# Routed experts of a small decoder: the expert's weights as the stationary operand of the gate and up products

## The chip, the cores and the metric

The kernel runs on one core of a Trainium2 chip. The metric is the device time of one execution in microseconds (us), lower is better. The engines that matter here are TensorE (PE in the profile, its weight loads PEld), VectorE (DVE), ScalarE (ACT), GpSimd (POOL) and SyncE (SP), which issues most transfers. Each engine has a sequencer of its own that takes its instructions in program order; the profile writes it with a q behind the engine's name (PEldq is TensorE's).

## The reference

Two decoder layers over x of 8 x 512 tokens with 256 channels: attention, cross attention and a feed-forward part each. The part that the change touches is the last one, a mixture of experts over all 4096 tokens:

```
logits = xt @ router_w.T + routing_bias          # 8 experts
topk_p, topk_idx = top_k(sigmoid(logits), 2)     # normalised to sum 1
g = einsum('th,eih->tei', xt, wg)                # H = 256 -> I = 512
u = einsum('th,eih->tei', xt, wu)
y = einsum('tei,ehi->teh', silu(g) * u, wd)      # I = 512 -> H = 256
routed = einsum('te,teh->th', w, y)
x = x + shared + routed
```

## The kernel before

The kernel works in phases, one after the other: attention of layer 0, cross attention, feed-forward, the same of layer 1, and last `experts_phase`. That phase has three parts. First, for each of the 8 batches, the shared expert is computed, the router chooses two experts for each token, and each token's row is scattered to a place of its expert in the DRAM tensor `xs`. Second comes the **block loop**: `xs` is read in NK = 71 blocks of 128 rows, each of one expert, and each block goes through its expert. Third, the two weighted results of each token are read back from the DRAM tensor `yd` and added to x.

All of an expert's values are held as two float16 halves, a high and a low one, so every product is three matmuls for each 128 values summed over: high x high, low x high, high x low. `wall` holds the weights of all 8 experts in SBUF, high part (q = 0) and low part (q = 1). Which expert a block belongs to is known only at run time. So `weight_base` (line 2557) reads the expert's offset from the table `wtab` into a register of TensorE's sequencer, and every access to `wall` in the block loop has an address that is that register plus a constant. The address is worked out in a sequencer instruction of its own just ahead of the matmul that needs it; successive matmuls on the same piece of `wall` share one.

A block k passes these steps in the kernel before:

- `block_turn` (TensorE): 4 transposes of 128 columns turn the rows `xr` of the block into bank 0; VectorE copies them to `xb` (line 2431).
- `block_gate_up` (TensorE): gate and up products, 12 matmuls of 512 columns. The block's tokens are stationary and the weights stream, so that the result has tokens on partitions and the 512 inner values along the free axis. Banks 2 and 3 or 4 and 5 take them.
- `block_squash` (ScalarE, line 2241) makes `sg` from the gate bank, VectorE makes `h` (line 2439), `block_high` (ScalarE, line 2245) its high half `hb`, VectorE its low half `lb` (line 2444). The tiles `hb` and `lb` are called `mo_hh` and `mo_hl` in the trace.
- `block_turn_hidden` (TensorE, line 2575): 8 transposes of 128 columns turn `hb` and `lb` into bank 1, and `block_turned` (ScalarE, line 2251) copies them to `hT`, since the down product sums over the inner values, which have to lie on partitions.
- `block_down` (TensorE): 12 matmuls of 256 columns, `hT` stationary, weights streaming. VectorE scales the result by the token's share (line 2450), GpSimd writes the rows to `yd` with an indirect transfer (line 2188).

TensorE's order in the loop is written out by hand: in round k it takes `block_turn(k + 2)`, `weight_base(k + 1)`, `block_gate_up(k + 1)`, `block_turn_hidden(k)`, `block_down(k - 1)`. All matmuls of the products stand on line 161, in the helper `product`, and so do the sequencer instructions that work out their addresses. In the trace the matmuls of the block loop are the ones named `ps<-mo_wall,mo_xt` (`hT` and `xb` are both views of the tile `mo_xt`).

Of the kernel before, what the change touches and what calls it, by code (L numbers as in the profile page):

```python
# [25 lines left out]
ALU = mybir.AluOpType  # L26
ACT = mybir.ActivationFunctionType
# [3 lines left out]
P = 128  # L31
NJ = T // P
NC = D // P
# [66 lines left out]
def banks(r, first, n=1):  # L100
    return r.ps[:, first * BANK:(first + n) * BANK]
# [56 lines left out]
def product(nc, out, terms):  # L158

    for n, (lhs, rhs) in enumerate(terms):  # L160
        last = nc.tensor.matmul(out, lhs, rhs, start=(n == 0), stop=(n == len(terms) - 1))  # L161
    return last
# [1864 lines left out]
E_, FI = 8, 512  # L2027
NI = FI // P
NW = NC * FI
# [8 lines left out]
def experts_phase(nc, r, d, out, nb=B):  # L2038
# [3 lines left out]
    with ExitStack() as es:  # L2042
        sb = lambda n, s, t=F32: es.enter_context(nc.sbuf_tensor(f"{tag}_{n}", s, t))
        sem = lambda n: new_semaphore(nc, r, f"{tag}_{n}")
        norm = Norm(nc, es, tag, r)
        wall = sb("wall", [P, E * EW], F16)
# [3 lines left out]
        xt = sb("xt", [P, 2, 2, NC * T], F16)  # L2050
        sg, h = sb("sg", [P, 2, FI]), sb("h", [P, 2, FI])
# [4 lines left out]
        ident16, tri, onesb = sb("ident16", [P, P], F16), sb("tri", [P, P], BF16), sb("onesb", [P, P], BF16)  # L2056
# [19 lines left out]
        gn = norm.xn[:].rearrange("p j c -> p (j c)")[:, 0:NBLK * E].rearrange("p (k e) -> p k e", e=E)  # L2076
        yt = norm.xn
        xb = xt[:, 0].rearrange("p a (b c) -> p (a b) c", c=2 * NC * P)
        hT = xt[:, 1]
        hb, lb = hh, hl  # L2080
        yb = wall[:, 0:8 * 4 * BT].bitcast(F32).rearrange("p (b k c) -> p b k c", k=2, c=BT)

# [7 lines left out]
        scattered = [sem(f"scattered{i}") for i in range(3)]  # L2090
        (tail_ready, tab_ready, padded) = (sem(n) for n in ("tail_ready", "tab_ready", "padded"))
        row_in = [sem(f"row_in{i}") for i in range(NR)]
        (bt_done, xb_ready, bgu_done, bsg_ready, bh_ready, bhh_ready, bhl_ready, ht_done, ht_ready, bdn_done, y_ready, picked, id_ready) = (
            sem(n) for n in ("bt_done", "xb_ready", "bgu_done", "bsg_ready", "bh_ready", "bhh_ready", "bhl_ready", "ht_done", "ht_ready", "bdn_done",
                             "y_ready", "picked", "id_ready"))
        y_out = [sem(f"y_out{i}") for i in range(4)]
        (y0_in, y1_in, sum_ready, stored) = ([sem(f"y0_in{b}") for b in range(nb)], [sem(f"y1_in{b}") for b in range(nb)], sem("sum_ready"), sem("stored"))
# [1 line left out]
        GU = ((2, 3), (4, 5))  # L2099
        DN = 6  # L2100
        NK = NBLK
        part_of = lambda s, p: sh[:, p].rearrange("p n w -> p (n w)") if s == 0 else wall[:, (s - 1) * EW + p * 3 * NW:(s - 1) * EW + (p + 1) * 3 * NW]
        xt_view = lambda b, p: xt[:, b % 2, p].rearrange("p (c t) -> p c t", c=NC)
        half_bank = lambda bank: banks(r, bank).bitcast(F16)
# [86 lines left out]
        @block.scalar  # L2191
        def _(act):
            def split(s):
                act.wait_ge(w_in, 48 * (s + 1))
                for n in range(3):
                    act.activation(part_of(s, 0)[:, n * NW:(n + 1) * NW], stage[:, n, :], ACT.Copy, scale=WS).then_inc(w_hi, 1)

            def high(b):
                act.wait_ge(norm.xn_ready, b + 1)
                if b >= 3:  # L2200
                    act.wait_ge(scattered[b % 3], 16 * 2 * NJ * (b // 3))
                act.activation(xw[:, b % 3, :, 0:D], norm.xn[:], ACT.Copy).then_inc(hi_ready, 1)

            def high_turned(b):
                act.wait_ge(th_done, b + 1)
                act.activation(xt[:, b % 2, 0], half_bank(0), ACT.Copy).then_inc(xth_ready, 1)

            def sigmoid(b):
                act.wait_ge(lg_ready, b + 1)
                act.activation(pr[:], lg[:], ACT.Sigmoid).then_inc(pr_ready, 1)  # L2210

            def squash(b, i):
                n = b * NI + i
                act.wait_ge(gu_done, n + 1)
                act.activation(sg[:, i % 2, :], banks(r, GU[i % 2][0]), ACT.Silu, scale=1.0 / WS).then_inc(sg_ready, 1)  # L2215
                act.wait_ge(h_ready, n + 1)
                act.activation(hh[:, i, :], h[:, i % 2, :], ACT.Copy).then_inc(hh_ready, 1)  # L2217

            act.wait_ge(rw_in, 16)
            act.activation(rwh[:], w32[:], ACT.Copy, scale=WS).then_inc(rw_hi, 1)  # L2220
            high(0)
            high_turned(0)
            sigmoid(0)
            high(1)
            split(0)
            for b in range(nb):
                squash(b, 0)
                squash(b, 1)
                if b + 1 < nb:
                    high_turned(b + 1)  # L2230
                squash(b, 2)
                squash(b, 3)
                if b + 1 < nb:
                    sigmoid(b + 1)
                if b + 2 < nb:
                    high(b + 2)
                split(b + 1)

            def block_squash(k):
                act.wait_ge(bgu_done, k + 1)  # L2240
                act.activation(sg[:, k % 2, :], banks(r, GU[k % 2][0]), ACT.Silu, scale=1.0 / WS).then_inc(bsg_ready, 1)  # L2241

            def block_high(k):
                act.wait_ge(bh_ready, k + 1)
                act.activation(hb[:, k % 2, :], h[:, k % 2, :], ACT.Copy).then_inc(bhh_ready, 1)  # L2245

            def block_turned(k):
                act.wait_ge(ht_done, k + 1)
                if k >= 2:
                    act.wait_ge(bdn_done, k - 1)  # L2250
                act.activation(hT[:, k % 2, :], half_bank(1), ACT.Copy).then_inc(ht_ready, 1)  # L2251

            block_squash(0)
            block_high(0)
            for k in range(NK):
                if k + 1 < NK:
                    block_squash(k + 1)
                block_turned(k)
                if k + 1 < NK:
                    block_high(k + 1)  # L2260
            act.wait_ge(bdn_done, NK)
            for i in range(4):
                act.wait_ge(y_out[i], 16 * len(range(i, NK, 4)))
            for b in range(nb):
                act.dma_start(yb[:, b, 1, :].rearrange("p (j c) -> p j c", c=D),
                              yd[B * T + b * T:B * T + (b + 1) * T].rearrange("(j p) c -> p j c", p=P)).then_inc(y1_in[b], 16)

        @block.vector
        def _(ve):
# [167 lines left out]
            def block_hidden(k):  # L2437
                ve.wait_ge(bsg_ready, k + 1)
                ve.scalar_tensor_tensor(out=h[:, k % 2, :], in0=banks(r, GU[k % 2][1]), scalar=1.0 / WS, in1=sg[:, k % 2, :],  # L2439
                                        op0=ALU.mult, op1=ALU.mult).then_inc(bh_ready, 1)  # L2440
                ve.wait_ge(picked, k + 1)
                ve.tensor_scalar(idu[:, k % 8:k % 8 + 1], wid[:, k % 8, 1:2], spare[:, k:k + 1], None, ALU.add).then_inc(id_ready, 1)
                ve.wait_ge(bhh_ready, k + 1)
                ve.tensor_tensor(lb[:, k % 2, :], h[:, k % 2, :], hb[:, k % 2, :], ALU.subtract).then_inc(bhl_ready, 1)  # L2444

            def block_out(k):
                ve.wait_ge(bdn_done, k + 1)
# [24 lines left out]
        def _(pe):  # L2472
# [86 lines left out]
            def block_gate_up(k, at):  # L2559
                pe.wait_ge(xb_ready, k + 1)  # L2560
                if k >= 2:
                    pe.wait_ge(bh_ready, k - 1)
                x = lambda p, c: xb[:, k % 4, (p * NC + c) * P:(p * NC + c + 1) * P]
                w = lambda n, q, c: wall[:, bass.ds(at + (q * 3 * NW + n * NW + c * FI), FI)]
                for n in range(2):
                    last = product(nc, banks(r, GU[k % 2][n]), [(x(p, c), w(n, q, c)) for c in range(NC) for p, q in ((0, 0), (1, 0), (0, 1))])
                last.then_inc(bgu_done, 1)

            def block_turn_hidden(k):
                if k:  # L2570
                    pe.wait_ge(ht_ready, k)
                for p, (src, ready) in enumerate(((hb, bhh_ready), (lb, bhl_ready))):
                    pe.wait_ge(ready, k + 1)
                    for i in range(NI):
                        last = nc.tensor.transpose(half_bank(1)[:, (p * NI + i) * P:(p * NI + i + 1) * P], src[:, k % 2, i * P:(i + 1) * P], ident16[:])  # L2575
                last.then_inc(ht_done, 1)

            def block_down(k, at):
                pe.wait_ge(ht_ready, k + 1)
                if k >= 2:  # L2580
                    pe.wait_ge(y_ready, k - 1)
                x = lambda p, i: hT[:, k % 2, (p * NI + i) * P:(p * NI + i + 1) * P]
                w = lambda q, i: wall[:, bass.ds(at + (q * 3 * NW + 2 * NW + i * D), D)]
                product(nc, banks(r, DN + k % 2)[:, 0:D],
                        [(x(p, i), w(q, i)) for i in range(NI) for p, q in ((0, 0), (1, 0), (0, 1))]).then_inc(bdn_done, 1)
# [8 lines left out]
            for k in range(NK):  # L2594
                if k + 2 < NK:
                    block_turn(k + 2)
                if k + 1 < NK:
                    bases.append(weight_base(k + 1))
                    block_gate_up(k + 1, bases[k + 1])
                block_turn_hidden(k)  # L2600
                if k:
                    block_down(k - 1, bases[k - 1])
            block_down(NK - 1, bases[NK - 1])
# [19 lines left out]
```

## Time and profile before

| | |
|---|---|
| time, median of 3 runs | 2194.77 us (2186.49 to 2195.98) |
| the profiled execution, its time | 2192.16 us |
| its span (first to last instruction) | 2190.4 us |
| TensorE busy | 1699.3 us, 78% of the span |
| VectorE busy | 1330.0 us, 61% |
| ScalarE busy | 1115.3 us, 51% |
| GpSimd busy | 921.2 us, 42% |
| block loop, first turn to last product | about 1818 to 2149 us of the span |

```text
span 2190.4 us, 35961 instructions
## 1 busy us (share of the span) xinstructions
PE 1699.3 (78%) x12334; PEld 865.6 (40%) x12350; DVE 1330.0 (61%) x3662; ACT 1115.3 (51%) x1530; POOL 921.2 (42%) x942
## 2 busy tenths in 40 slices
PE   4988888888688894677777774577748888999992
PEld 2222222222255562233333332244325555666661
DVE  2777777774377983356666654354348875555554
ACT  2366677666356993245555541354425553444441
POOL 3135555422368414357777553354424341222220
PEclk9999999999789997579998866699969998999996
DMA  4333233320200001433333300522213332222217
GB/s 99 63 69 58 57 56 54 50 45 1 70 1 1 1 1 38 64 50 50 50 50 50 50 2 24 65 56 57 42 59 112 118 132 84 59 60 59 62 51 242
DMA packets 117859, 126.65 MB, mean 58 GB/s; under 512 B 21684, under 2 KB 104116, under 8 KB 117652
## 3 DMA queue, kind: packets, MB, share of 16 engines
q1 hardware_dynamic: 106980, 101.94, 23.8%
q0 software_dynamic: 6480, 18.23, 2.2%
q10 hardware_dynamic: 4224, 4.19, 0.6%
q8 instruction: 105, 1.72, 0.3%
q14 instruction: 70, 0.57, 0.1%
HBM read 77.94 MB, written 45.16 MB: 56 GB/s over the span
## 5 line engine op out<-in xcount | busy, mean ns | idle before, releaser
L634 ACT ACTIVATE at_pexp<-ps 128x1024 f32<-128x1024 f32 (+3 forms) x480 | 385.5, 826 | 198.3 <-PE ps L867 197.5
L695 DVE TENSOR_REDUCE at_mx<-ps 128x1 f32<-128x512 f32 x512 | 323.8, 683 | 140.1 <-PE ps L874 138.4
L874 PE MATMUL ps<-at_ks,at_qs 48*128 48x512 f16 (+3 forms) x1024 | 293.5, 361 | 93.0 <-DVE at_mx L695 41.6
L161 PE MATMUL ps<-mo_wall,mo_xt 128*128 x1704 | 302.4, 328 | 0.9 <-issue 0.9
L867 PE MATMUL ps<-at_qs,at_ks 50*128 50x512 f16 (+4 forms) x1024 | 252.9, 345 | 28.3 <-DMA at_qs<-at_mhl 22.5
L927 PE MATMUL ps<-at_pexp,at_vaug 128*32 128x512 f32 (+4 forms) x2048 | 224.1, 532 | 8.0 <-issue 7.0
L161 PEld LDWEIGHTS ps<-mo_wall,mo_xt 128*128 128x128 f16 x1704 | 161.2, 98 | 95.0 <-issue 4.3
L2188 POOL DMA_INDIRECT mo_yd<-mo_xn,mo_idu x71 | 68.1, 959 | 272.5 <-DVE mo_xn L2450 263.3
L697 DVE CUSTOM_DVE_ANT_0 at_junk<-ps,at_lmask 128x192 bf16<-128x192 f32 x384 | 115.4, 352 | 85.0 <-PE ps L874 84.1
L874 PEld LDWEIGHTS ps<-at_ks,at_qs 48*128 48x128 f16 x1024 | 76.0, 98 | 213.5 <-DVE at_mx L695 123.1
L2241 ACT ACTIVATE mo_sg<-ps 128x512 f32<-128x512 f32 x71 | 42.4, 597 | 195.2 <-PE ps L161 195.2
L867 PEld LDWEIGHTS ps<-at_qs,at_ks 50*128 50x128 f16 x1024 | 70.7, 98 | 172.0 <-issue 87.4
L2439 DVE SCALAR_TENSOR_TENSOR mo_h<-ps,mo_sg 128x512 f32<-128x512 f32 x71 | 49.1, 691 | 105.1 <-ACT mo_sg L2241 105.1
L492 POOL TENSOR_TENSOR at_qkl<-at_qk,at_qkh 128x512 f16<-128x512 f32 x64 | 78.0, 1218 | 71.7 <-ACT at_qk L618 69.0
L161 PE MATMUL ps<-mo_xt,mo_sh 128*128 128x512 f16 x384 | 88.9, 386 | 12.3 <-DVE mo_sh L2283 8.6
L539 POOL TENSOR_TENSOR at_pexp<-at_pexp,at_keep_l 128x768 int32<-128x768 int32 x48 | 92.2, 1929 | 14.1 <-ACT at_pexp L634 14.1
L697 DVE CUSTOM_DVE_ANT_0 at_junk<-ps,at_cmask 128x512 bf16<-128x512 f32 (+3 forms) x128 | 57.5, 487 | 59.9 <-PE ps L874 58.0
L2183 POOL DMA_INDIRECT mo_xs<-mo_xw,mo_slotu x64 | 64.3, 1005 | 68.4 <-DVE mo_slotu L2340 51.4
L927 PEld LDWEIGHTS ps<-at_pexp,at_vaug 128*32 128x32 f32 x2048 | 49.1, 116 | 76.3 <-issue 62.2
L2444 DVE TENSOR_TENSOR mo_hl<-mo_h,mo_hh 128x512 f16<-128x512 f32 x71 | 49.1, 692 | 44.0 <-ACT mo_hh L2245 44.0
L2251 ACT ACTIVATE mo_xt<-ps 128x1024 f16<-128x1024 f16 x71 | 72.3, 1018 | 1.2 <-PE ps L2575 1.2
L161 PE MATMUL ps<-ff_wq,ff_xqt 128*128 128x512 bf16 x240 | 64.3, 384 | 9.5 <-DVE ff_h L1354 5.0
(395 smaller groups left out, 3768.8 us busy)
## 6 DMA issues: line engine op xcount, KB each, us to landing
at_qs<-at_scratch SPq DMA_DIRECT2D x96, 128.0 KB, 7.0
at_ks<-at_scratch SPq DMA_DIRECT2D x96, 128.0 KB, 7.7
mo_xr<-mo_xs SPq DMA_DIRECT2D x71, 136.0 KB, 2.3
at_scratch<-at_qkh SPq DMA_DIRECT2D x64, 128.0 KB, 1.8
at_scratch<-at_qkl SPq DMA_DIRECT2D x64, 128.0 KB, 1.8
x_qs<-x_qscratch SPq DMA_DIRECT2D x48, 128.0 KB
mo_stage<-in_m_gate SPq DMA_DIRECT2D x9, 512.0 KB, 3.9
mo_stage<-in_m_up SPq DMA_DIRECT2D x9, 512.0 KB, 4.7
```

Source lines behind the costliest of these rows:

```text
L161: last = nc.tensor.matmul(out, lhs, rhs, start=(n == 0), stop=(n == len(terms) - 1))
L492: pool.tensor_tensor(qkl[:, m, :], qk32[:, m, :], qkh[:, m, :], ALU.subtract).then_inc(qkl_ready, 1)
L539: pool.tensor_tensor(part.bitcast(I32), part.bitcast(I32), kept, ALU.mult).then_inc(pool_masked, 1)
L634: last = act.activation(columns(pexp[:, U % 2, hh], at, n, stride, width), columns(banks(r, ST[S % 2], 2), at, n, stride, width), ACT.Exp, ...
L695: last = ve.reduce_max(out, score, AX.X)
L697: last = ve.tensor_tensor_reduce(junk[:, i % 3, piece.at:piece.at + piece.n], score, piece.mask[:, 0:piece.n], 1.0, NEG, ALU.add, ALU.max, ...
L867: return nc.tensor.matmul(banks(r, ST[(b * K + k) % 2], 2)[:, piece.at:piece.at + piece.n], ks[rows, b % 2, h // 2, piece.idx * P:(piece.i ...
L874: return nc.tensor.matmul(banks(r, MX[i % 2])[:, piece.at:piece.at + piece.n], qs[rows, (n // 2) % 2, h // 2, piece.idx * P:(piece.idx + 1 ...
L927: last = nc.tensor.matmul(banks(r, O)[32 * hh:32 * hh + 32, piece.lo:piece.lo + piece.n], vaug[:, b % 2, piece.idx, h, :], pexp[:, (b * NU ...
L2183: pool.indirect_dma_start(xs[:], bass.IndirectOffsetOnAxis(ap=slotu[:, b, k * NJ + j:k * NJ + j + 1], axis=0), rows(b % 3)[:, j, :], None) ...
L2188: pool.indirect_dma_start(yd[:], bass.IndirectOffsetOnAxis(ap=idu[:, k % 8:k % 8 + 1], axis=0), yt[:, k % 4, :], None).then_inc(y_out[k % ...
L2251: act.activation(hT[:, k % 2, :], half_bank(1), ACT.Copy).then_inc(ht_ready, 1)
```

## The change

The gate and up products change their operands' places. The stationary operand is now a piece of the expert's weights of 128 columns, and the block's tokens stream, 128 columns. A product of 128 inner values is 6 matmuls; there are 4 such pieces (NI = 4) in each of gate and up, so `block_gate_up` has 48 matmuls of 128 columns. The result has inner values on partitions and tokens along the free axis, 4 pieces side by side in the same bank. `hb` and `lb` therefore have already the form that the down product's stationary operand wants. `block_turn_hidden`, `block_turned`, the tile view `hT` and the semaphores `ht_done` and `ht_ready` are gone; `block_down` waits on `bhl_ready` in their place, and `hb` and `lb` take 4 buffers instead of 2, with a wait of ScalarE for the down product of four blocks before.

```diff
@@ ScalarE
-                act.activation(hb[:, k % 2, :], h[:, k % 2, :], ACT.Copy).then_inc(bhh_ready, 1)
-
-            def block_turned(k):
-                act.wait_ge(ht_done, k + 1)
-                if k >= 2:
-                    act.wait_ge(bdn_done, k - 1)
-                act.activation(hT[:, k % 2, :], half_bank(1), ACT.Copy).then_inc(ht_ready, 1)
-
-            block_squash(0)
-            block_high(0)
+                if k >= 4:
+                    act.wait_ge(bdn_done, k - 3)
+                act.activation(hb[:, k % 4, :], h[:, k % 2, :], ACT.Copy).then_inc(bhh_ready, 1)
+
             for k in range(NK):
-                if k + 1 < NK:
-                    block_squash(k + 1)
-                block_turned(k)
-                if k + 1 < NK:
-                    block_high(k + 1)
+                block_squash(k)
+                block_high(k)
...
@@ TensorE
-                w = lambda n, q, c: wall[:, bass.ds(at + (q * 3 * NW + n * NW + c * FI), FI)]
+                w = lambda n, q, c, i: wall[:, bass.ds(at + (q * 3 * NW + n * NW + c * FI + i * P), P)]
                 for n in range(2):
-                    last = product(nc, banks(r, GU[k % 2][n]), [(x(p, c), w(n, q, c)) for c in range(NC) for p, q in ((0, 0), (1, 0), (0, 1))])
+                    for i in range(NI):
+                        last = product(nc, banks(r, GU[k % 2][n])[:, i * P:(i + 1) * P],
+                                       [(w(n, q, c, i), x(p, c)) for c in range(NC) for p, q in ((0, 0), (1, 0), (0, 1))])
                 last.then_inc(bgu_done, 1)
 
-            def block_turn_hidden(k):
-                if k:
-                    pe.wait_ge(ht_ready, k)
-                for p, (src, ready) in enumerate(((hb, bhh_ready), (lb, bhl_ready))):
-                    pe.wait_ge(ready, k + 1)
-                    for i in range(NI):
-                        last = nc.tensor.transpose(half_bank(1)[:, (p * NI + i) * P:(p * NI + i + 1) * P], src[:, k % 2, i * P:(i + 1) * P], ident16[:])
-                last.then_inc(ht_done, 1)
-
             def block_down(k, at):
-                pe.wait_ge(ht_ready, k + 1)
+                pe.wait_ge(bhl_ready, k + 1)
                 if k >= 2:
                     pe.wait_ge(y_ready, k - 1)
-                x = lambda p, i: hT[:, k % 2, (p * NI + i) * P:(p * NI + i + 1) * P]
+                x = lambda p, i: (hb, lb)[p][:, k % 4, i * P:(i + 1) * P]
...
-                block_turn_hidden(k)
                 if k:
                     block_down(k - 1, bases[k - 1])
```

What stands in a row on TensorE, of one round in the middle of the block loop. The rows named ISA on line 161 are the sequencer instructions that work out an address in `wall` (the trace calls them FUSED_REGOPS); TENSOR_LOAD reads the table. Before, the start of the gate and up products (the pattern of the last four rows repeats until 12 matmuls and 8 ISA rows stand there):

```order
L2553 MATMUL ps<-mo_ident,mo_xr 128x128 x4
L2557 TENSOR_LOAD mo_wtab
L2557 ISA x2
L161 ISA
L161 MATMUL ps<-mo_wall,mo_xt 128x512 x2
L161 ISA
L161 MATMUL ps<-mo_wall,mo_xt 128x512
```

The same place now (the pattern of the last four rows repeats until 48 matmuls and 32 ISA rows stand there):

```order
L2547 TENSOR_LOAD mo_wtab
L2547 ISA x2
L161 ISA
L161 MATMUL ps<-mo_xt,mo_wall 128x128 x2
L161 ISA
L161 MATMUL ps<-mo_xt,mo_wall 128x128
```

Each streams a quarter of the columns, there are four times as many of them, and the address instructions are four times as many too. The second place is TensorE from the end of the gate and up products to the start of the down product. Before:

```order
L161 ISA
L161 MATMUL ps<-mo_wall,mo_xt 128x512
L2575 MATMUL ps<-mo_ident,mo_hh 128x128 x4
L2575 MATMUL ps<-mo_ident,mo_hl 128x128 x4
L161 ISA
L161 MATMUL ps<-mo_wall,mo_xt 128x256 x2
L161 ISA
L161 MATMUL ps<-mo_wall,mo_xt 128x256
```

Now:

```order
L161 ISA
L161 MATMUL ps<-mo_xt,mo_wall 128x128
L161 ISA
L161 MATMUL ps<-mo_wall,mo_hh 128x256
L161 MATMUL ps<-mo_wall,mo_hl 128x256
L161 ISA
L161 MATMUL ps<-mo_wall,mo_hh 128x256
```

The 8 transposes are gone. The down product keeps its 12 matmuls and 8 address instructions.

## Rows read from the trace of the kernel before

**Rows 1.** The page: granted clock of TensorE in tenths, 40 slices.

```profile
PEclk9999999999789997579998866699969998999996
```

**Rows 2.** Busy time by stretch: shared experts, block loop; then granted clock, DMA share.

```profile
core 0: us, PE busy (x) PEld busy (x) DVE busy (x) ACT busy (x) POOL busy (x), PEclk, DMA share, GB/s
1699.50:1740.40 40.90, 32.96 (x261) 20.10 (x259) 32.94 (x96) 21.50 (x29) 14.51 (x16) 1.00 0.33 120
...
1829.76:2136.00 306.24, 306.24 (x2413) 202.28 (x2414) 166.15 (x470) 136.57 (x203) 63.27 (x66) 1.00 0.21 59
```

**Rows 3.** The chain that ended last, within one round: start, us, what.

```profile
1976.17 2.59 PE ps L161 x12
1978.76 0.45 PE ps L2575 x8
1979.21 1.31 PE ps L161 x12
1980.52 0.22 PE ps L2553 x4
```

**Rows 4.** Line 161, TensorE's loads and sequencer, 1820.27 to 1821.12 us; then 1820.28 to 1821.11.

```profile
L161 PEldq FUSED_REGOPS  x8: 42/46/51, 1820.2 to 1821.1; - x8
...
L161 PEldq FUSED_REGOPS  x6: 46/46/51, 1820.4 to 1821.0; - x6
```

**Rows 5.** The same view, 1829.6 to 1830.5 us.

```profile
L161 PEldq FUSED_REGOPS  x7: 42/46/46, 1829.7 to 1830.4; - x7
```

**Rows 6.** The loop's first rounds in order of time, TensorE.

```profile
1820.33 5.30 PE L161 MATMUL ps<-mo_wall,mo_xt 128*128 x12 [0.42 <-issue]
1825.42 0.57 PE L2553 MATMUL ps<-mo_ident,mo_xr 128*128 128x128 f16 x4
1825.83 2.75 PE L161 MATMUL ps<-mo_wall,mo_xt 128*128 x12
...
1828.86 0.39 PE L2553 MATMUL ps<-mo_ident,mo_xr 128*128 128x128 f16 x4
1829.76 0.60 PE L161 MATMUL ps<-mo_wall,mo_xt 128*128 x2 [0.51 <-issue]
```

**Rows 7.** TensorE's sequencer by source line, 1828.7 to 1831.5 us, outside line 161.

```profile
L2551 PEldq EVENT_SEMAPHORE  x1: 51/51/51, 1828.7 to 1828.7; - x1
...
L2557 PEldq TENSOR_LOAD <-mo_wtab x1: 304/304/304, 1828.9 to 1828.9; - x1
L2557 PEldq FUSED_REGOPS  x1: 151/151/151, 1829.3 to 1829.3; - x1
L2557 PEldq SEQ_ASSERT  x1: 18/18/18, 1829.5 to 1829.5; - x1
...
L2573 PEldq EVENT_SEMAPHORE  x1: 51/51/51, 1830.8 to 1830.8; - x1
```

**Rows 8.** The loop's end in order of time, TensorE.

```profile
2142.89 0.39 PE L2575 MATMUL ps<-mo_ident,mo_hh 128*128 128x128 f16 x4
...
2146.14 2.63 PE L161 MATMUL ps<-mo_wall,mo_xt 128*128 x22
```

**Rows 9.** Groups by line and form, 1830 to 2136 us: count, busy us, mean ns, idle before.

```profile
L2251 ACT ACTIVATE mo_xt<-ps 128x1024 f16<-128x1024 f16 x68 | 69.2, 1018 | 0.0
L2188 POOL DMA_INDIRECT mo_yd<-mo_xn,mo_idu x66 | 63.3, 959 | 260.5 <-DVE mo_xn L2450 251.7 <-issue 8.8
...
L2439 DVE SCALAR_TENSOR_TENSOR mo_h<-ps,mo_sg 128x512 f32<-128x512 f32 x67 | 46.3, 691 | 95.9 <-ACT mo_sg L2241 95.9
```

**Rows 10.** The router's products of 8 columns in order of time, TensorE: 21 starts later.

```profile
1670.03 0.17 PE L161 MATMUL ps<-mo_rwl,mo_xt 128*128 128x8 f16 x1
...
1670.56 0.17 PE L161 MATMUL ps<-mo_rwl,mo_xt 128*128 128x8 f16 x1
```

**Rows 11.** Transposes of float32, 128 columns, in order of time, TensorE.

```profile
1321.14 0.63 PE L815 MATMUL ps<-ident,at_ot 128*128 128x128 f32 x4 [0.88 <-DVE X L753]
```

**Rows 12.** Line 815 over the whole span: ns of one, shortest, median, longest.

```profile
L815 PE MATMUL ps<-ident,at_ot x256: 272/273/476, 158.1 to 1326.7; 128*128 128x128 f32 x128
```

More of the change, by code:

```diff
@@ L2078, in experts_phase @@
         xb = xt[:, 0].rearrange("p a (b c) -> p (a b) c", c=2 * NC * P)
-        hT = xt[:, 1]
         hb, lb = hh, hl
@@ L2092, in experts_phase @@
         row_in = [sem(f"row_in{i}") for i in range(NR)]
-        (bt_done, xb_ready, bgu_done, bsg_ready, bh_ready, bhh_ready, bhl_ready, ht_done, ht_ready, bdn_done, y_ready, picked, id_ready) = (
-            sem(n) for n in ("bt_done", "xb_ready", "bgu_done", "bsg_ready", "bh_ready", "bhh_ready", "bhl_ready", "ht_done", "ht_ready", "bdn_done",
+        (bt_done, xb_ready, bgu_done, bsg_ready, bh_ready, bhh_ready, bhl_ready, bdn_done, y_ready, picked, id_ready) = (
+            sem(n) for n in ("bt_done", "xb_ready", "bgu_done", "bsg_ready", "bh_ready", "bhh_ready", "bhl_ready", "bdn_done",
                              "y_ready", "picked", "id_ready"))
@@ L2443, in block_hidden @@
                 ve.wait_ge(bhh_ready, k + 1)
-                ve.tensor_tensor(lb[:, k % 2, :], h[:, k % 2, :], hb[:, k % 2, :], ALU.subtract).then_inc(bhl_ready, 1)
+                ve.tensor_tensor(lb[:, k % 4, :], h[:, k % 2, :], hb[:, k % 4, :], ALU.subtract).then_inc(bhl_ready, 1)
             def block_out(k):
```

## The prediction

> **What bounds the kernel now.** I read the page first, then the chain that ended last, since the change touches one loop only. The page's clock row gives nine tenths or more in the slices of that loop [rows 1]. The busy times by stretch say it plainly: from 1829.76 to 2136 us TensorE is busy for 306.24 of 306.24 us at granted clock 1.00, with ScalarE at 136.57 us, VectorE at 166.15 us and GpSimd at 63.27 us [rows 2]. So TensorE sets the pace of the loop and no other engine is near. The chain shows what a round is made of [rows 3]: 2.59 us for the 12 gate and up matmuls of 512 columns (0.216 us each), 0.45 us for 8 transposes of `hb` and `lb` (0.056 each), 1.31 us for the 12 matmuls of 256 columns of the down product (0.109 each), 0.22 us for 4 transposes of the block's rows (0.056 each). The sum is 4.57 us, with nothing between them.
>
> By columns alone the change looks like a gain. But TensorE has a second resource, its sequencer, and the view of single source lines shows it. So that is the view I looked at longest. At 1820 us the array runs at half clock and the sequencer is free to go ahead; there its 8 address instructions of one gate and up product, with the 12 matmuls and 12 weight loads between them, are gone through between 1820.2 and 1821.1 us [rows 4]. The two windows bracket it: the first instruction ends between 1820.27 and 1820.28 and lasted 42 ns, the eighth starts between 1821.11 and 1821.12. That is 0.87 to 0.89 us for seven steps, 0.124 to 0.127 us for one. One more stretch at full clock: 7 instructions from 1829.7 to 1830.4 [rows 5], 0.12 a step. In the same two places the matmuls themselves take 5.1 us (1820.33 to 1825.42) and 2.59 us [rows 3, 6]. Before, then, the sequencer needs 8 x 0.124 = 0.99 us for what the array takes 2.59 us over, and the address work is hidden under 512-column matmuls.
>
> **The change part by part.**
>
> *The array's work.* Removed are 8 transposes, 0.45 us. The gate and up products keep their columns (12 x 512 = 48 x 128). The price of a matmul of 128 float16 columns with a weight load of its own is that of the transposes, 0.056 us: 12 of them take 0.67 us of each round [rows 3]. 48 x 0.056 = 2.67 us in place of 2.59. Down stays 1.31, the rows' transposes 0.22. The array needs 4.20 us a round, 0.37 less than now. It is bounded by a nearer and a farther row: a weight load with only 8 columns behind it repeats every 0.025 us (0.53 us for 21 starts) [rows 10], so loading does not hinder at 0.056; float32 transposes of 128 columns come (0.63 - 0.27) / 3 = 0.12 us apart [rows 11, 12], which would be 5.76 us for 48. I take 0.056, since load, type and columns are the same.
>
> The Trainium skill ("TensorE: Matmul & The Clock Gate", section "Back-to-back issue gap") says that a stream of weight load and matmul pairs sustains about 81 ns a matmul at 128 columns. By that figure the estimate for the array is 48 x 0.081 + 1.31 + 4 x 0.081 = 5.5 us a round. This trace has 0.056 us for such pairs, at most 12 in a row, and the measurement decides; a run of 48 is not in it.
>
> *The sequencer's work.* This is the term that counts. There are 32 address instructions in a gate and up product where there were 8, and 48 matmuls where there were 12: the mix is the same, 2 to 3. So whether the 0.124 us belongs to the address instruction or to what stands between does not matter: the same mix, four times. 32 x 0.124 = 3.97 us. The rest of a round on the sequencer: from the wait at the head of `block_turn` (1828.7) over the table read (1828.9), the register work on it (1829.3) and the bounds check (1829.5) [rows 7] to the first address instruction of the product (1829.7 [rows 5]; its matmul starts at 1829.76 [rows 6]): 0.92 us with the 4 transposes in it. That this time is real the array shows too: it stands idle for 0.51 us ahead of 1829.76 with "issue" named as the cause [rows 6]. Then a wait for the down product, about 0.11 us (an event instruction lasts 51 ns [rows 7], and the next comes after one step), and its 8 address instructions, 0.99 us. Sum 0.92 + 3.97 + 0.11 + 0.99 = 5.99; the table's read varies by a few hundredths, and I take **5.98 us a round**. Before, the same sum is 0.92 + 0.99 + 0.11 + 0.99 plus the transposes' waits, about 3.1 of 4.57 us, hidden. After, 5.98 stands against the array's 4.20, and the sequencer is what sets the end: +1.41 us a round.
>
> *A register address on the weight load.* Before, the matmul carries it and the load has a fixed one; after it is the reverse. No row shows the new form. The nearest are the old one, where it costs no more than the 0.124 us step (0 extra), and, were it to drop to the slow load of float32, the 0.12 us above. It could also be cheaper by nothing more than those steps hold. I take 0.
>
> *ScalarE, VectorE and waits.* ScalarE loses a copy of 1.018 us a block, VectorE keeps its work [rows 9]. Both have room (45% and 54% busy in a shorter round [rows 2]), so that is worth 0. `block_down(k - 1)` now waits on the low half `lb` of block k - 1, whose products ended a full round before; behind that wait stand the next round's transposes and table read, and the first to suffer would be TensorE itself. From product to `lb` there are four elementwise passes; at the 0.69 us of VectorE's [rows 9] each that is 2.8 us, and a round of 5.98 covers it. The wait of ScalarE for the down product of four blocks before is met by rounds. GpSimd's transfer, 0.96 us a block [rows 9], is covered as well.
>
> *Edges.* The first product runs at half clock for 5.1 us in both forms, the columns being equal, so it hides its own 3.97. The sequencer then reaches the product of block 2 about 0.4 us later than now. From there to the product of block 70 are 68 rounds: 68 x 1.41 = 95.9. That last product takes 1.4 us longer. After it, now 5.88 us pass to the last matmul (2142.89 to 2148.77 [rows 8]), with the transposes and the copy of the last two blocks in them; then it is three down products, 3 x 1.31 and a hand-over, 4.1 us: -1.8. Sum 95.9 + 0.4 + 1.4 - 1.8 = **+96 us**.
>
> The profiled execution took 2192.2 us, of which 2190.4 are span; 2192.2 + 96 = 2288. The median of the three runs is 2.6 us above it, so I say **2290 us**.
>
> **The rivals.**
>
> *A. The array stays the bound* (the address work is hidden as it is now, or the sequencer goes faster through the short matmuls). For it: it is hidden now. Against it: 5 to 6 us of sequencer work in 4.2 us of array time, measured with the array out of the way. Price: 68 x (4.20 - 4.57) = -25, and -1.8 at the end: 2167 us, faster. It would need a step below 0.08 us ((4.57 - 1.03) / 40 = 0.089 for no change). Chance 5 in 100.
>
> *B. The weight load becomes slow*, because of its register address or because 48 in a row is more than 12 in a row. At 0.12 us the array needs 5.76 + 1.31 + 0.22 = 7.29 us a round, 68 x 2.72 + 2 = +187: 2382 us. It decides only from (5.98 - 1.53) / 48 = 0.093 us on; below that, the sequencer hides it. Chance 6. The 0.081 us of the Trainium skill's page lies below that point, so by it this rival would not show.
>
> *C. The clock falls.* TensorE gets gaps: it would stream for 4.20 of 5.98 us. At half clock the array needs 2 x 4.20 = 8.4 us, and 2.4 more a round. For it: the page has slices at five to eight tenths [rows 1], in phases with pauses. Against it: in the shared experts TensorE is busy 32.96 of 40.9 us and keeps 1.00 [rows 2]. If a fifth of the rounds ran so, 14 x 2.4 = +34: 2324 us. Chance 7.
>
> *D. The edit does not do what it says*: ruled out, the order shows the transposes gone and the 32 address instructions in place. Small departures (another step length, a better round) are in the forecast's own range.
>
> **How the numbers follow.** Forecast 80 in 100, C 7, B 6, A 5, others 2, spread around. Own range of the forecast: 5.9 to 6.1 us a round is -5 to +8 us, and the runs before spread from -8 to +1 around their median: 2278 to 2302. To hold 8 in 10 with the margins of this case, the range goes down a little for a cheaper round and up into C: 2270 to 2325. A measurement of this kernel tells some 0.5% (11 us) from no change. Faster by more than that is A, 0.05; within it, 0.01; slower, 0.94.
>
> **What would show it.** In the new profile a round should take 5.9 to 6.1 us on the chain, with "issue" named ahead of matmuls; the address instructions of line 161 stand 0.124 us apart through the whole round, 40 a round; matmuls of the gate and up products come in a pattern, 3 to 0.25 us, which is two steps; clock 1.00; ScalarE's copy gone and its wait for TensorE longer. If the address instructions stand farther apart than 0.13 us with the array busy, B is right; if the granted clock has fallen in the loop, C; if they are closer and the round is near 4.2, A. The forecast would be wrong above all if the step of 0.124 us grew or shrank once the load, not the matmul, carries the register.

## The result and the profile after

The changed kernel takes 2307.20 us (median of 4 runs, 2306.26 to 2310.99) against 2191.65 us (4 runs, 2186.49 to 2195.98) of the kernel before: a ratio of 1.054, 95% interval 1.051 to 1.057. It is slower by 116 us; 96 were forecast. The ratios in this document are estimates from the single runs (two runs of the kernel before in a slower state, of the 15 in one series, are left out), so they differ in the third digit from the quotient of the medians beside them.

The profiled execution took 2306.26 us, 114 more than that of before. The page of the changed kernel, span and busy times, then the granted clock in 40 slices:

```profile
span 2304.5 us, 41498 instructions
...
PE 1798.9 (78%) x14322; PEld 987.6 (43%) x14338; DVE 1333.0 (58%) x3662; ACT 1058.0 (46%) x1459; POOL 921.0 (40%) x942
...
PEclk8699999998889976698888667998799899999996
```

VectorE kept its time. ScalarE has lost 57 us: its 71 copies of 1.018 us are 72 us, but each overlapped the operations beside it by about 0.1 us at both ends. TensorE's busy time has grown by 100 us though it does fewer columns: busy counts a matmul's way through the array, and a short one lasts 0.225 us by its row while the next starts 0.09 us after it in the mean of a product (4.35 us for 48), so they still overlap. By stretch (last columns granted clock, DMA share, GB/s) the loop now looks so; the answering rows of before are [rows 2]:

```profile
core 0: us, PE busy (x) PEld busy (x) DVE busy (x) ACT busy (x) POOL busy (x), PEclk, DMA share, GB/s
...
1829.76:2250.00 420.24, 402.89 (x4285) 316.79 (x4283) 166.30 (x469) 82.16 (x134) 63.74 (x67) 1.00 0.15 43
```

The clock is 1.00 as before, VectorE and GpSimd do the same work in more time, ScalarE does its work without the copy, and TensorE is no longer busy all the time. The chain within a round, start, us, what; the rows of before are [rows 3]:

```profile
1981.62 1.48 PE ps L161 x12
1983.10 0.22 PE ps L2543 x4
1983.32 0.27 issue
1983.60 4.12 PE ps L161 x47
1987.71 0.01 issue
1987.72 0.23 PE ps L161
1987.95 0.00 issue
1987.95 1.48 PE ps L161 x12
```

A round is 6.33 us here and 6.28 at the median. The 0.45 us of transposes are gone, and the gate and up products take 4.35 us instead of 2.59. What spreads them is in the view of line 161 from 1983.4 to 1987.7 us, one gate and up product, to be compared with [rows 4, 5]:

```profile
L161 PEldq FUSED_REGOPS  x32: 42/46/46, 1983.5 to 1987.6; - x32
```

32 address instructions in 4.1 us, one each 0.13 us, from the first matmul to the last. Each lasts 46 ns by its row; what fills the rest of the 0.13 us no view shows. Among all waits in the loop (1830 to 2250 us) TensorE's own is for nothing but its issue, and who waits for TensorE waits longer:

```profile
ACT mo_sg L2240 <- PE ps L161: 286.5, 67, 4.4
...
PE ps L161 <- issue: 15.4, 68, 0.4
```

One thing in these totals is not the loop's. The loop's first transposes start at different times in the two profiled executions, though all that runs ahead of them is the same code. Before, then now:

```profile
1818.13 0.58 PE L2553 MATMUL ps<-mo_ident,mo_xr 128*128 128x128 f16 x4 [8.86 <-DMA mo_xr<-mo_xs]
```

```profile
1814.50 0.59 PE L2543 MATMUL ps<-mo_ident,mo_xr 128*128 128x128 f16 x4 [7.21 <-DMA mo_xr<-mo_xs]
```

From there to the end of the span it is 372.3 us before and 490.0 now: the change costs 117.7 us in this pair of executions, and 3.6 us of it are hidden by a shorter stretch ahead of the loop. In the eight profiled executions of this case that stretch takes 1811 to 1831 us. So small differences are better read from the loop's first transpose on than from the whole time.

### The profile page after: what moved, and what is told of

It is laid out like the page before. It is cut to its first block and busy times, and to the rows that moved or that the text cites. A ratio compares the mean times of both kernels' runs of the same rounds, so it can differ in the third digit from the quotient of the medians.

```text
span 2304.5 us, 41498 instructions
## 1 busy us (share of the span) xinstructions
PE 1798.9 (78%) x14322; PEld 987.6 (43%) x14338; DVE 1333.0 (58%) x3662; ACT 1058.0 (46%) x1459; POOL 921.0 (40%) x942
## 3 DMA queue, kind: packets, MB, share of 16 engines
q8 instruction: 127, 2.08, 0.4%
## 5 line engine op out<-in xcount | busy, mean ns | idle before, releaser
L161 PE MATMUL ps<-mo_xt,mo_wall 128*128 128x128 f16 x3408 | 307.0, 226 | 17.9 <-issue 16.4
L161 PEld LDWEIGHTS ps<-mo_xt,mo_wall 128*128 x3408 | 239.0, 97 | 88.6 <-issue 35.5
L161 PE MATMUL ps<-mo_wall,mo_hh 128*128 x568 | 105.2, 274 | 1.3 <-DVE mo_xn L2440 0.6
L161 PE MATMUL ps<-mo_wall,mo_hl 128*128 x284 | 77.4, 273 | 0.0
```

## Experiments

The theory: TensorE's sequencer sets the pace, by about 0.124 us for each address instruction. The rivals were that the short matmuls or their weight loads are slow in themselves, and that a register address costs more on the weight load than on the matmul.

**Fixed addresses in the changed kernel.** Every access to `wall` in the block loop gets a fixed address, the one of expert 0, so all tokens go through expert 0; the table is still read.

```diff
-                w = lambda n, q, c, i: wall[:, bass.ds(at + (q * 3 * NW + n * NW + c * FI + i * P), P)]
+                w = lambda n, q, c, i: wall[:, q * 3 * NW + n * NW + c * FI + i * P:q * 3 * NW + n * NW + c * FI + i * P + P]
...
-                w = lambda q, i: wall[:, bass.ds(at + (q * 3 * NW + 2 * NW + i * D), D)]
+                w = lambda q, i: wall[:, q * 3 * NW + 2 * NW + i * D:q * 3 * NW + 2 * NW + i * D + D]
```

> The changed kernel with every access to the experts' weights in the block loop at a fixed address (always expert 0, so the routed part's values are those of expert 0 for all tokens); the table read stays, the 40 address instructions a round are gone, matmuls and loads are the same. Theory (TensorE's sequencer sets the pace): the array is the bound again, a round takes 48 x 0.056 + 1.31 + 0.22 = 4.2 us and the time is about 2165 us, below the kernel before. Rival (a row of 48 weight loads and short matmuls is slow in itself): a round stays near 6.3 us and the time near 2305 us.

Measured: 2165.94 us against 2194.37 us, ratio 0.989 (0.984 to 0.994). The chain within a round:

```profile
1975.46 0.22 PE ps L2543 x4
1975.69 3.99 PE ps L161 x60
1979.68 0.22 PE ps L2543 x4
1979.90 3.99 PE ps L161 x60
```

60 matmuls in 3.99 us with no "issue" between them, a round of 4.21: 2.67 for the 48 short ones if the 12 of the down product keep their 1.31, so 0.056 us each. The array's part of the forecast (4.20) stands, a run of 48 loads and short matmuls is no slower than a run of 12, and all that makes the changed kernel slow leaves with the 40 address instructions. From the loop's first transpose (1817.07 us) to the end of the span it is 346.8 us, 25.5 less than in the kernel before.

**Fixed addresses in the kernel before.** The same edit on the other kernel.

```diff
-                w = lambda n, q, c: wall[:, bass.ds(at + (q * 3 * NW + n * NW + c * FI), FI)]
+                w = lambda n, q, c: wall[:, q * 3 * NW + n * NW + c * FI:q * 3 * NW + n * NW + c * FI + FI]
...
-                w = lambda q, i: wall[:, bass.ds(at + (q * 3 * NW + 2 * NW + i * D), D)]
+                w = lambda q, i: wall[:, q * 3 * NW + 2 * NW + i * D:q * 3 * NW + 2 * NW + i * D + D]
```

> The kernel before with the same edit: fixed weight addresses in the block loop (always expert 0), 16 address instructions a round gone. Theory: they were hidden under 512-column matmuls, so the round stays at 4.57 us and the time at 2192 us, within 0.3%. Rival (address instructions cost the array something each, 0.043 us as in the changed kernel's surplus of 1.7 us for 40): 16 x 0.043 = 0.7 us a round less, about 2145 us.

Measured: 2200.92 us against 2194.37 us, ratio 1.0035 (0.999 to 1.008). One round on the chain, to the next one's start:

```profile
1979.17 2.59 PE ps L161 x12
1981.76 0.45 PE ps L2575 x8
1982.20 1.31 PE ps L161 x12
1983.51 0.22 PE ps L2553 x4
```

It is the round of [rows 3], 4.57 us. So 16 address instructions a round cost nothing there: whatever they take is hidden behind the long matmuls. The forecast for the total was 2192 us, no change, and the ratio's interval holds 1. The profiled execution is 12 us longer than that of before, and all of it stands ahead of the loop: the first transpose starts at 1831.01 us, and from there it is 371.4 us to the end, against 372.3.

**The old operand order in short matmuls.** In the kernel before each 512-column matmul is cut into four; the register stays on the streaming operand, the tokens' weight load has a fixed address, and the transposes stay.

```diff
-                w = lambda n, q, c: wall[:, bass.ds(at + (q * 3 * NW + n * NW + c * FI), FI)]
+                w = lambda n, q, c, i: wall[:, bass.ds(at + (q * 3 * NW + n * NW + c * FI + i * P), P)]
...
-                    last = product(nc, banks(r, GU[k % 2][n]), [(x(p, c), w(n, q, c)) for c in range(NC) for p, q in ((0, 0), (1, 0), (0, 1))])
+                    for i in range(NI):
+                        last = product(nc, banks(r, GU[k % 2][n])[:, i * P:(i + 1) * P],
+                                       [(x(p, c), w(n, q, c, i)) for c in range(NC) for p, q in ((0, 0), (1, 0), (0, 1))])
```

> The kernel before, operands in their old places (tokens stationary at a fixed address, weights streaming at a register address), but each 512-column matmul of gate and up cut into four of 128 columns: 48 matmuls and 32 address instructions, and the 8 transposes stay. Theory: the number of address instructions decides, whichever operand carries the register: 1.03 + 40 x 0.124 + about 0.3 = 6.3 us a round, time about 2313 us. Rival (the register address on the weight load is what is slow): the array bounds at 48 x 0.056 + 1.31 + 0.67 = 4.65 us, about 2197 us.

Measured: 2316.52 us (one run). One product on the chain:

```profile
1980.06 0.06 issue
1980.13 4.12 PE ps L161 x47
1984.24 0.01 issue
1984.26 0.23 PE ps L161
```

4.35 us for a gate and up product with the register on the matmul, and 4.35 us in the changed kernel with the register on the weight load. Over the whole loop the mean step within such a train is 0.133 us here and 0.132 there, from the starts in the two traces. Which operand carries the register makes no difference; the number of addresses does. The round is 6.45 us at the median (6.3 expected), 0.17 longer than the changed kernel's: the transposes are still there, and about 0.12 us of it lies between the last address instruction of this product and the first of the down product, where their waits stand. This also settles that the operand swap is not at fault. Its cutting into pieces is.

**More address instructions, the same matmuls.** In the changed kernel the low x high term reads a piece of its own, from the down weights, so that its value is not the layer's; 56 address instructions a round instead of 40.

```diff
+                v = lambda n, c, i: wall[:, bass.ds(at + (2 * NW + 16 + (n * 8 + i * 2 + c) * 32), P)]
...
-                                       [(w(n, q, c, i), x(p, c)) for c in range(NC) for p, q in ((0, 0), (1, 0), (0, 1))])
+                                       [(v(n, c, i) if p else w(n, q, c, i), x(p, c)) for c in range(NC) for p, q in ((0, 0), (1, 0), (0, 1))])
```

> The changed kernel, but the low x high term of gate and up reads a weight piece of its own (from the down weights, so that term's values are not the layer's) in place of the piece of the term ahead of it: same 60 products and 4 transposes a round, 56 address instructions for 40. Theory: a step of 0.124 us for each address instruction: 6.28 + 16 x 0.124 = 8.3 us a round, time about 2442 us. Rival (the step belongs to the matmul and load pairs between them): the round stays at 6.3 us, 2307 us. On the longer steps of 0.15 to 0.3 us that come after every eighth address instruction in the changed kernel: if they come by instructions gone through (32 of all kinds), they come now after 10 to 11 address instructions; if by address instructions, still after 8.

Measured: 2461.24 us (one run), round 8.36 us at the median. The gate and up product on the chain, then line 161 in the same stretch (1980.6 to 1987.05 us, the last of the 49 is the down product's first):

```profile
1980.48 0.29 issue
1980.77 6.24 PE ps L161 x48
...
L161 PEldq FUSED_REGOPS  x49: 42/46/46, 1980.7 to 1986.9; - x49
```

48 matmuls now take 6.24 us, 0.130 us each, one for each address instruction. The total is 19 us above the 2442 expected: 8 us of it stand ahead of the loop, whose first transpose starts at 1822.49 us here, and the rest is for the most part a mean step above 0.124 and the longer first and last products. With 16 more of them the round is 8.36 - 6.28 = 2.08 us longer, 0.130 us for one. The pairs of load and matmul between them are the same 48, so the step belongs to the address instruction. (No run has two address instructions with nothing between them, so the price of one by itself is not measured.)

This run was also to tell what the longer steps count. In the changed kernel seven steps of 0.124 are followed by a longer one, so that the address instructions come in groups of eight. The view of line 161 in four short windows, two successive groups of the changed kernel and two of this one:

```profile
L161 PEldq FUSED_REGOPS  x8: 46/46/46, 1984.4 to 1985.3; - x8
...
L161 PEldq FUSED_REGOPS  x8: 46/46/46, 1985.4 to 1986.3; - x8
...
L161 PEldq FUSED_REGOPS  x8: 46/46/46, 1906.9 to 1907.7; - x8
...
L161 PEldq FUSED_REGOPS  x8: 46/46/46, 1907.9 to 1908.8; - x8
```

Both have groups of 8, though 12 load and matmul pairs lie in a group of the changed kernel and 8 in one of this. So the longer step is tied to the address instructions and not to all instructions gone through, which would have made it 10 or 11. These two kernels alone can't tell eight instructions from a stretch of about 1 us, as both take steps of 0.124. The traces can: in the long trains (24 address instructions and more in a row) of the changed kernel, this one, the short matmuls in the old order and the version with two pieces below, 875 of 876 distances between successive longer steps are eight address instructions, though such a group lasts anything from 1.02 to 1.18 us. A cause that came by the clock would slip against the count. What happens in the longer step was not found.

**One piece of four, and two of four, in the new order.** The kernel before with the first m pieces of gate and up in the new order and the rest in the old; only the rest is turned. The code is written here with m; the two kernels have 1 and 2 in its place.

```diff
...
-                w = lambda n, q, c: wall[:, bass.ds(at + (q * 3 * NW + n * NW + c * FI), FI)]
+                w = lambda n, q, c: wall[:, bass.ds(at + (q * 3 * NW + n * NW + c * FI + m * P), FI - m * P)]
+                s = lambda n, q, c, i: wall[:, bass.ds(at + (q * 3 * NW + n * NW + c * FI + i * P), P)]
...
+                    for i in range(m):
+                        product(nc, banks(r, GU[k % 2][n])[:, i * P:(i + 1) * P],
+                                [(s(n, q, c, i), x(p, c)) for c in range(NC) for p, q in ((0, 0), (1, 0), (0, 1))])
+                    last = product(nc, banks(r, GU[k % 2][n])[:, m * P:FI], [(x(p, c), w(n, q, c)) for c in range(NC) for p, q in ((0, 0), (1, 0), (0, 1))])
...
-                    for i in range(NI):
+                    for i in range(m, NI):
...
+                x = lambda p, i: (hb, lb)[p][:, k % 4, i * P:(i + 1) * P] if i < m else hT[...]
```

> The kernel before with the new operand order for one of the four 128-column pieces of gate and up (6 transposes of the hidden values left of 8, 12 short and 12 384-column matmuls, 24 address instructions a round). Theory: sequencer 1.03 + 24 x 0.124 + 0.2 = 4.2 us, array 0.67 + 1.94 + 1.31 + 0.56 = 4.48 us, so the array bounds and a round is 0.09 us shorter than 4.57: about 2185 us, 0.3% faster than the kernel before. Rival (the short matmuls locally outrun the sequencer, since the queue ahead of the array is not deep enough to bridge them): a round of 4.7 us or more, 2200 us or more.

> The same with two of the four pieces in the new order: 4 transposes left, 24 short and 12 256-column matmuls, 32 address instructions a round. Theory: sequencer 1.03 + 32 x 0.124 + 0.25 = 5.2 us, array 1.34 + 1.31 + 1.31 + 0.45 = 4.41 us: the sequencer bounds at 5.2 us, about 2237 us. Rival (time goes with the array's work and a fixed loss for each short matmul, 1.7 us over 48): 4.57 + 24 x 0.035 = 5.4 us, 2249 us.

Measured with one piece: 2183.49 us (12 runs) against 2188.58 us (17 runs), ratio 0.9983 (0.9966 to 1.0000). With two: 2239.13 us (one run). A round of the first, and one of the second, on the chain:

```profile
1980.70 2.62 PE ps L161 x24
1983.33 0.33 PE ps L2581 x6
1983.66 1.31 PE ps L161 x12
1984.97 0.22 PE ps L2555 x4
```

```profile
1977.34 0.11 issue
1977.45 3.49 PE ps L161 x36
1980.94 0.22 PE ps L2581 x4
1981.16 1.31 PE ps L161 x12
1982.47 0.22 PE ps L2555 x4
```

With one piece the array bounds: 2.62 + 0.33 + 1.31 + 0.22 = 4.48 us, the forecast to the hundredth, and nothing stands between. With two the sequencer does: a round of 5.37 us at the median, with "issue" on the chain, against an array need of 4.41. That round lies nearer to the rival's 5.4 us (a fixed loss of 0.035 us for each short matmul) than to the 5.2 expected, so this run alone doesn't decide between them. The one with one piece does: by the rival its 12 short matmuls would make a round of 4.57 + 0.42 = 4.99 us, and it takes 4.49. The crossing lies between 24 and 32 address instructions a round, where it was put. The version with one piece is the only one here that computes the layer's values and comes in below the kernel before, by 0.2%, at the edge of what 12 runs can tell. The loop shows it more clearly: 0.08 us less a round over 68 rounds is 5.6 us, and from the loop's first transpose to the end of the span its trace has 366.4 us against 372.3.

| kernel | address instructions a round | round, us | who bounds |
|---|---|---|---|
| fixed, before | 0 | 4.57 | array |
| fixed, changed | 0 | 4.21 | array |
| before | 16 | 4.57 | array |
| one piece | 24 | 4.49 | array |
| two pieces | 32 | 5.37 | sequencer |
| changed | 40 | 6.28 | sequencer |
| before in short matmuls | 40 | 6.45 | sequencer |
| changed, own addresses | 56 | 8.36 | sequencer |

## Why the forecast held, point by point

The measured 2307 us lie in the stated range of 2270 to 2325, and the mechanism is the forecast one. But the forecast's own range, from a round of 5.9 to 6.1 us to 2278 to 2302 us, missed both the round (6.28) and the time. What brought the time inside is the part of the range that was added for a falling clock, and no clock fell: that much is luck.

**What bounds the loop.** It said that TensorE's sequencer takes the array's place. Shown: with the address instructions taken away the changed kernel falls to 4.21 us a round, and with more of them and the same matmuls it rises.

**The array's part.** 4.20 us forecast, 4.21 measured where nothing else is in the way. The Trainium skill's 81 ns a matmul at 128 columns ("TensorE: Matmul & The Clock Gate", "Back-to-back issue gap") does not hold here: 60 matmuls in 3.99 us leave 0.056 us for each short one, in a run of 48.

**The sequencer's part.** 5.98 us forecast, 6.28 measured, and this is the term that was mis-sized. From the starts of the sequencer's instructions in the trace, in the mean of 62 rounds: from `block_turn`'s wait to the first address instruction 0.90 us (0.92 in the sum), the 32 steps 4.24 (3.97), the wait 0.11 (0.11), the down product's 8 steps 1.03 (0.99). So the overhead was right and the step was short: 0.132 us in the mean for a long train. The two stretches that the 0.124 was read from [rows 4, 5] have 8 and 7 instructions, just too few to hold one of the longer steps that come with every eighth. 0.30 us over 68 rounds is 20 us, and 96 + 20 = 116 against the 117.7 measured from the loop's first transpose on. The prediction's sign for rival B, address instructions farther apart than 0.13 us, is met by this mean of 0.132 without B being right: it left no room for a longer step among seven of 0.124.

**The register on the weight load.** Put at 0 extra; the short matmuls in the old order show 4.35 us for the same product, so it is 0 as far as the trace can tell.

**Engines beside it.** Put at 0. ScalarE's copy is gone (busy 1115.3 to 1058.0 us) and that is worth nothing in either kernel, as it now waits for TensorE instead (4.3 us a block).

**The edges.** Put at 0.0 in sum (0.4 + 1.4 - 1.8). Against the 114 us of the whole time, 68 x 1.71 = 116 seems to leave -2; but the stretch ahead of the loop was 3.6 us shorter, and of the 117.7 us behind it 1.5 are the edges'. By the starts in the two traces, counted from the first gate and up product, block 2's product starts 0.6 us later (0.4 forecast), the last product takes 1.8 us longer (1.4), from its end to the last matmul it is 1.2 us less (1.8), and 0.3 us lie behind that. The 1.2 falls short of the 1.8 because the last down product waits:

```profile
2261.31 0.28 PE L161 MATMUL ps<-mo_wall,mo_hh 128*128 x1 [0.59 <-DVE mo_xn L2440]
```

**The rivals.** A (array stays the bound) would have needed the sequencer to work under short matmuls faster than under the long ones at half clock [rows 4]; it does not. B had two forms: that 48 loads in a row are slow fell with the fixed addresses (0.056 us each), that a register address makes the load slow fell with the old order in short matmuls, which is as slow with the register on the other operand. C (a falling clock) did not come: 1.00 through the loop, with TensorE's gaps in it.

## What to carry to other kernels

On TensorE here, an operand whose address is only known at run time costs an instruction in the engine's own sequencer (0.13 us in the mean), and that is a second resource with its own sum: count the addresses a round, and set their time against the array's time for the same round. Cutting long matmuls into short ones multiplies the first and leaves the second, so a change that saves array work can lose. It is worth looking for a stretch in the old profile where the array is held up by something else, since the sequencer's own pace shows there; but it must be a long one: here one of 8 instructions gave 0.124 us, and the mean over trains of 32 is 0.132.

## What the runs showed of the hardware

- An address instruction (FUSED_REGOPS) lasts 46 ns by its row and costs 0.124 us in a train, with one or with two pairs of load and matmul behind it; those cost nothing beside it. With 56 instead of 40 a round, one costs 0.130 us.
- Every eighth step of such a train is longer, 0.15 to 0.3 us (0.18 to 0.19 in the mean), which makes the mean step 0.131 to 0.133. It goes by the address instructions, not by all instructions (groups of eight with 12 and with 8 load and matmul pairs) and not by time (groups of 1.02 to 1.18 us). Its cause stays open.
- Matmuls of 128 float16 columns with a load each run 0.056 us apart in a row of 48, with clock 1.00 (the changed kernel with fixed addresses: 3.99 us for 48 of them and 12 of 256 columns).
- The same short matmuls spread over 6.3 us a round did not lower the granted clock: 1.00 from 1829.76 to 2250 us.
- With 24 address instructions a round the array still bounds (4.49 us), with 32 no longer (5.37 us).
